# Flamingo block on one core: the opening reordered, the mask as a selection matrix, the hi and lo split of Wq by column blocks, K spread by SBUF-to-SBUF loads, the value projection in two halves

## The chip, the cores and the metric

One core of one Trainium2 chip. A core has TensorE (matmuls, here PE, with the loading of its stationary operand as PEld), VectorE (DVE), ScalarE (ACT), GpSimd (POOL) and SyncE (SP), each with its own queue of instructions, and 16 engines that move data (DMA). SyncE and ScalarE issue all transfers here. The metric is the device time of one execution in microseconds, lower is better. Before the change it is 689.58 us, the median of three runs (688.52 to 692.12).

## The reference

The block adds a gated cross attention and then a gated feed-forward part to `x`, which is 2 batches of 2048 rows of 512. The context is 77 rows of 384 for each batch, with a mask over these 77 rows.

```
q = (layernorm(x) @ Wq)   k = (context @ Wk)   v = (context @ Wv)    # 16 heads of 32
scores = einsum('bhid,bhjd->bhij', q, k) * scale
scores = where(context_mask, scores, -finfo.max);  attn = softmax(scores)
x = x + tanh(g_xattn[0]) * (einsum('bhij,bhjd->bhid', attn, v) @ Wo)
xq = fake_quant(layernorm(x));  gate = xq @ quant(w_gate).T;  up = xq @ quant(w_up).T
h = fake_quant(silu(gate) * up)
x = x + tanh(g_ffn[0]) * (h @ quant(w_down).T)
```

## The kernel before

The kernel has three blocks, one after the other: attention (to about 413 us), gate and up projection (to about 599 us), and down projection. The change lies in the opening of the first.

Attention works on 32 tiles of 128 rows. A matmul with full precision is made of three: each operand is split into a rounded part and the rest (`_hi`, `_lo`), and `three` multiplies hi by hi, hi by lo and lo by hi. For each tile of x, VectorE makes the statistics (`stats_both`), GpSimd the factors (`deviation`), ScalarE the normalised row (`normalise`), TensorE its transposes (`x_transpose`), and ScalarE and VectorE take these apart into hi and lo (`x_part`). `queries(m, t, part)` works on two tiles together, and for one column block of Wq at a time: tile number 0 does blocks 0 and 1, number 1 blocks 2 and 3. `q_part` splits what comes out.

Each engine's work is an order written out by hand: an opening, and then `tile_slots`, which runs `slot` once for each tile. In slot n TensorE does the scores of tile n, the transposes of the probabilities of tile n-1 and its outputs, queries for tile n+2, transposes of x for tile n+4, and the projection of tile n-2. Engines wait for one another by semaphores only.

The opening prepares keys and values. `c_sb` is the context, `cT` its transposes (L869), `cK` a version for the keys in which every masked row is replaced by the first row that is kept (L648 to L674; then a masked row's score is no larger than the maximum, and its value is made zero by `keepT`). The keys are 12 matmuls into `p_k` (L876). K stands in the scores as a block matrix, `k_hi` and `k_lo`, zero except for each head's own 32 rows; GpSimd fills both with zeros (L379, L380), ScalarE writes eight blocks of `k_hi` (L475) and VectorE eight of `k_lo` (L692). The values (L886) are scaled by the gate and by `keepT` into `v_sb` (L704), and SyncE spreads them by twelve loads from SBUF to SBUF into `vblk` (L323), which GpSimd has filled with zeros (L381).

`v_sb` lies in the buffer `pT`, into which ScalarE copies the transposed probabilities. So ScalarE waits for all twelve loads in slot 1, ahead of those copies:

```
if isinstance(n, int) and n == 1:
    act.wait_ge(l_v, 16 * SLOT0[KB])
```

The order of TensorE in the opening is: transposes of the context, 24 matmuls that keep it busy (`keep_warm`), keys, transposes of tiles 0 and 1, both halves of the values, queries for tiles 0 and 1, transposes of tiles 2 and 3, slots. SyncE issues, in this order, the context, x tiles 0 and 1, Wk, Wq, x tiles 2 and 3, Wv, x tiles 4 to 7, the first rows of w_gate (`rows(0)`), then after its waits the twelve loads into `vblk`, `rows(1)`, Wo and x tiles 8 to 11. ScalarE issues the mask and the four gates, each spread over 128 partitions, ahead of its first work.

## Time and profile before

| | |
|---|---|
| median of three runs | 689.58 us (688.52 to 692.12) |
| span of the profiled execution | 689.8 us; nothing is listed around it, so this is taken as its own time |
| mean granted TensorE clock | 0.983 of full speed |
| busy share of the span | PE 94%, PEld 72%, DVE 74%, ACT 52%, POOL 24% |
| DMA, mean over the span | 77 GB/s |

The profile is of one execution. Its page gives the busy time of each engine, a timeline in 40 slices, the DMA queues, the chain of work that ended last, and the costliest groups of instructions. An engine's busy share is a mean over stages with different limits; a matmul's busy time overlaps that of the next. Times in the rows are microseconds from the start of the span.

### The profile page before, as it was taken

Reading aid. Unit: us, or ns where it says so; the run is one execution under the profiler, and the core shown is the slowest. Engines: PE = TensorE matmul, PEld = TensorE weight load, DVE = VectorE, ACT = ScalarE, POOL = GpSimd, SP = SyncE. Lnnn points to the kernel's source line nnn. Section 1 sums busy time; section 2 is a strip of 40 time slices with the busy share of each in tenths; the row PEclk is TensorE's granted clock in tenths of the full one; section 3 lists DMA queues with packets and bytes.
Section 4 is the critical chain, followed back from the end, with each engine's and each line's share of the span. In section 5 each row is a group of like instructions: output and inputs, shape, how many; then the busy total and the mean of one; then the engine's idle time right before and its main releaser. Section 6 shows DMA issues by size and latency. Waiting matters only on the chain. (4 is left out here: it accounts for less than half of the span.)

```text
span 689.8 us, 13450 instructions
## 1 busy us (share of the span) xinstructions
PE 649.7 (94%) x4207; PEld 493.7 (72%) x4233; DVE 509.4 (74%) x943; ACT 357.2 (52%) x561; POOL 166.9 (24%) x376
## 2 busy tenths in 40 slices
PE   6789999999999999999999992999999999898997
PEld 6588999999999999999999981444444444343443
DVE  4687878787878878777767652799778878846664
ACT  1555555555555655454543433578666664345553
POOL 5122223222222322211101110111111110026775
PEclk9999999999999999999999997799999999998999
DMA  7258000001010100000000004041244000089723
GB/s 233 75 169 321 32 17 27 21 15 30 15 30 15 30 15 31 2 1 1 1 1 1 1 1 167 1 168 58 111 169 167 0 0 1 21 304 322 284 106 122
DMA packets 22488, 53.29 MB, mean 77 GB/s; under 512 B 4884, under 2 KB 5038, under 8 KB 22446
## 3 DMA queue, kind: packets, MB, share of 16 engines
q1 hardware_dynamic: 16654, 35.96, 14.5%
q10 hardware_dynamic: 5792, 16.80, 6.9%
q8 instruction: 23, 0.38, 0.2%
q14 instruction: 19, 0.16, 0.1%
HBM read 32.50 MB, written 19.92 MB: 76 GB/s over the span
## 5 line engine op out<-in xcount | busy, mean ns | idle before, releaser
L523 DVE TENSOR_REDUCE sb_smax<-ps_s 128x8 f32<-128x616 f32 x64 | 51.1, 798 | 64.6 <-PE ps_s L760 64.4
L1150 PE MATMUL ps_g<-sb_xqT,sb_wgu 128*128 128x512 bf16 x338 | 90.0, 385 | 1.2 <-DVE sb_xqT L1122 0.5
L1150 PE MATMUL ps_u<-sb_xqT,sb_wgu 128*128 128x512 bf16 x349 | 90.8, 382 | 0.2
L1039 ACT ACTIVATE sb_silu<-ps_g,sb_sgu 128x512 f32<-128x512 f32 x88 | 60.5, 687 | 57.1 <-PE ps_g L1150 48.4
L1313 PE MATMUL ps_z<-sb_wdT,sb_hq 128*128 128x512 bf16 x344 | 78.8, 389 | 4.8 <-ACT sb_hq L1246 4.4
L422 ACT COPY sb_pT<-ps_p 128x512 f32<-128x512 f32 (+1 forms) x96 | 46.4, 521 | 70.1 <-PE ps_p L771 70.1
L1111 DVE SCALAR_TENSOR_TENSOR sb_h<-ps_u,sb_sgu,sb_silu 128x512 f32<-128x512 f32 (+1 forms) x88 | 66.0, 750 | 20.8 <-PE ps_u L1150 20.0
L721 PE MATMUL ps_q<-sb_xT_hi,sb_wq_hi 128*128 128x256 f32 x256 | 77.5, 303 | 2.0 <-DVE sb_q_lo L514 1.5
L782 PE MATMUL ps_o<-sb_vblk,sb_pT 128*128 (+4 forms) x640 | 79.0, 270 | 0.1
L782 PEld LDWEIGHTS ps_o<-sb_vblk,sb_pT 128*128 128x128 f32 (+1 forms) x640 | 76.8, 191 | 0.6 <-ACT sb_pT L422 0.3
L723 PE MATMUL ps_q<-sb_xT_hi,sb_wq_lo 128*128 128x256 f32 x256 | 72.4, 283 | 0.0
L722 PE MATMUL ps_q<-sb_xT_lo,sb_wq_hi 128*128 128x256 f32 x256 | 72.3, 282 | 0.0
L1313 PEld LDWEIGHTS ps_z<-sb_wdT,sb_hq 128*128 128x128 bf16 x352 | 35.0, 100 | 48.6 <-ACT sb_hq L1246 5.4
L1115 DVE TENSOR_REDUCE sb_hmax<-sb_h 128x1 f32<-128x512 f32 (+1 forms) x88 | 60.4, 686 | 7.6
L1150 PEld LDWEIGHTS ps_u<-sb_xqT,sb_wgu 128*128 128x128 bf16 x352 | 34.7, 99 | 42.5 <-issue 1.7
L1246 ACT CAST sb_hq<-sb_h 128x1408 bf16<-128x1408 int8 x32 | 43.6, 1365 | 40.9 <-DVE sb_h L1266 40.9
L410 ACT CAST sb_oT_hi<-ps_x 128x512 fp32r<-128x512 f32 x31 | 18.2, 588 | 88.6 <-PE ps_x L805 88.6
L1231 POOL TENSOR_TENSOR sb_wgu<-sb_wgu,sb_x 128x512 f32<-128x512 f32 x31 | 51.3, 1661 | 34.3 <-DVE sb_wgu L1272 17.6
L1150 PEld LDWEIGHTS ps_g<-sb_xqT,sb_wgu 128*128 128x128 bf16 x352 | 33.1, 99 | 34.7 <-issue 1.8
L529 DVE TENSOR_TENSOR sb_prob<-ps_s,sb_smax 128x616 f32<-128x616 f32 x64 | 51.1, 798 | 3.0
L721 PE MATMUL ps_y<-sb_wo_hi,sb_oT_hi 128*128 128x512 f32 x124 | 51.3, 414 | 0.9 <-DVE sb_wo_lo L605 0.9
L721 PEld LDWEIGHTS ps_q<-sb_xT_hi,sb_wq_hi 128*128 128x128 f32 x256 | 48.8, 191 | 2.8 <-issue 1.9
(154 smaller groups left out, 1373.8 us busy)
## 6 DMA issues: line engine op xcount, KB each, us to landing
h_spill<-sb_h SPq DMA_DIRECT2D x4, 2816.0 KB, 8.4
sb_h<-h_spill ACTq DMA_DIRECT2D x16, 704.0 KB, 6.0
out_dram<-sb_wgu SPq DMA_DIRECT2D x32, 256.0 KB, 2.0
sb_x<-in_x_dram ACTq DMA_DIRECT2D x1, 4096.0 KB, 15.6
sb_w_in<-in_L_ffn_w_gate_dram SPq DMA_DIRECT2D x11, 256.0 KB, 2.8
sb_w_in<-in_L_ffn_w_up_dram SPq DMA_DIRECT2D x11, 256.0 KB, 2.6
sb_h<-in_L_ffn_w_down_dram SPq DMA_DIRECT2D x4, 704.0 KB, 6.3
sb_x<-in_x_dram SPq DMA_DIRECT2D x2, 1024.0 KB, 11.8
```

Of the source, the lines that this page charges most:

```text
L523: dve.tensor_reduce(smax[:, half, :].rearrange("p (g h) -> p g h", g=2), half_scores(), X, ALU.max).then_inc(v_max, 1)
L529: dve.tensor_tensor(prob[t % 2][:, half, :].rearrange("p (g h m) -> p g h m", g=2, h=HG), half_scores(), smax[:, half, :].rearrange("p (g ...
L721: pe.matmul(o, hi, rhi, start=first, stop=False)
L722: pe.matmul(o, hi, rlo, start=False, stop=False)
L723: return pe.matmul(o, lo, rhi, start=False, stop=last)
L782: last = pe.matmul(p_o[:, first:end + 1, :].rearrange("p h d -> p (h d)"), pT[rows, half * KB + j, :], vblk[rows, span(b), half, SLOT0[j]: ...
L1039: act.activation(silu[(j * KI + i) % 2][:, :, :].rearrange("p t n -> p (t n)"), p_g[(j * KI + i) % 2][:, :], ACT.Silu, scale=sgu[:, i:i + ...
L1111: dve.scalar_tensor_tensor(steps_h, p_u[(j * KI + i) % 2][:, :, :], sgu[:, KI + i:KI + i + 1], silu[(j * KI + i) % 2][:, :, :], ALU.mult, ...
L1115: dve.tensor_reduce(hmax[:, span(u)], steps_h, mybir.AxisListType.XY, ALU.max, apply_absolute_value=True).then_inc(v_hmax, 1)
L1150: last = pe.matmul(banks[(j * KI + i) % 2][:, :], wgu[:, what, k, i * P:(i + 1) * P], xqT[j][:, k, :], start=(k == 0), stop=(k == KD - 1))
L1231: pool.tensor_tensor(yd[k], yd[k], x1[:, span((v + RT) % NT), :].rearrange("p a d -> p (a d)"), ALU.add).then_inc(g_out, 1)
L1313: last = pe.matmul(p_z[k % 4][:, :], hq[k % 4][:, i, :], wdT[:, i, :], start=(i == 0), stop=(i == KI - 1))
```

## The change

x tiles 0 and 1 are loaded ahead of the context. The mask comes in as one row, is spread over the partitions by a matmul with a row of ones (`p_m`), and transposed by two matmuls (`p_mT`); from both VectorE builds a 77 by 77 selection matrix for each batch (`pickw`), and TensorE multiplies the context by it to get `cK`. The four gates come in as one row as well and are spread by a matmul. ScalarE copies `cT`. GpSimd makes the ramps, and it fills `k_lo` and `vblk` with zeros only after the factors of tiles 0 and 1. Wq is split in four column blocks. The K halves are written whole into `kc_hi` and `kc_lo`, by one instruction each, and eight loads from SBUF to SBUF put them into `k_hi` and `k_lo`. The transposes of tile 1 stand between the halves of the keys. The values' first half stands between the queries of tile 0 and of tile 1, behind the transposes of tile 2; the second half behind the transposes of tile 3, at the end of the opening. The statistics of tile 3 move ahead on VectorE.

```diff
...
+kc_hi, kc_lo = [spare[:, (5 + 4 * i) * B * M:(9 + 4 * i) * B * M].bitcast(F32R)
+                .rearrange("p (b g m) -> p b g m", b=B, g=KD) for i in range(2)]
...
+p_ck = p_p[0][:, :, :].rearrange("p k n -> p (k n)")[:, 0:KC * B * M]\
+    .rearrange("p (k b m) -> p k b m", k=KC, b=B)
+p_m = p_ob[:, 0:B * M].rearrange("p (b m) -> p b m", b=B)
+p_mT = p_ob[0:M, 2 * P:2 * P + B]
+p_gate = p_ob[:, 3 * P:3 * P + 4]
...
+    sp.dma_start(x1[:, 0:2, :], x_v[:, 0:2, :]).then_inc(l_x[0], 16)
...
-    sp.dma_start(x1[:, 0:2, :], x_v[:, 0:2, :]).then_inc(l_x[0], 16)
...
+    sp.wait_ge(g_zero, 8)
+    for kc, k_blk, done in ((kc_hi, k_hi, a_khi), (kc_lo, k_lo, v_klo)):
+        sp.wait_ge(done, 1)
+        for j in range(HG):
+            rows_j = slice(HD * j, HD * j + HD)
+            sp.dma_start(k_blk[rows_j, :, :, M * j:M * j + M].bitcast(F32).rearrange("p b g m -> p (b g) m"),
+                         kc[rows_j, :, :, :].bitcast(F32).rearrange("p b g m -> p (b g) m")).then_inc(l_k, 16)
...
-    sp.wait_ge(g_zero, 9)
...
-    pool.iota(ramp_i[:, :, :], [[0, B], [-1, M]], M, 0).then_inc(g_zero, 1)
+    pool.memset(ones_row, 1.0).then_inc(g_ramp, 1)
+    pool.memset(eps[:, :], EPS).then_inc(g_zero, 1)
+    pool.iota(ramp_i[:, :, :], [[0, B], [-1, M]], M, 0).then_inc(g_ramp, 1)
+    pool.iota(rampT_i, [[0, 1]], M, -1).then_inc(g_ramp, 1)
...
-    pool.memset(eps[:, :], EPS).then_inc(g_zero, 1)
...
+    pool.wait_ge(g_ramp, 3)
+    pool.tensor_copy(ramp[:, :, :], ramp_i[:, :, :]).then_inc(g_ramp, 1)
+    pool.tensor_copy(rampT, rampT_i).then_inc(g_ramp, 1)
...
+    pool.wait_ge(g_zero, 6)
+    for n in range(2):
+        deviation(n, n)
...
-    pool.wait_ge(g_zero, 9)
-    for n in range(5):
+    for n in range(2, 5):
...
-            act.wait_ge(v_wq, 1)
+            act.wait_ge(v_wq, KD)
...
-    act.dma_start(mask_u[:, :, :], mask.rearrange("(a b) m -> a b m", a=1)
-                  .broadcast_to([P, B, M])).then_inc(l_mask, 16)
-    for b in range(B):
-        act.dma_start(maskT_u[:, b:b + 1], mask[b:b + 1, :].rearrange("b m -> m b"))\
-           .then_inc(l_maskT, 16)
+    act.dma_start(mask_u, mask.rearrange("(a b) m -> a (b m)", a=1)).then_inc(l_mask, 16)
...
-        act.dma_start(gates[:, i:i + 1], bcast(a)).then_inc(l_small, 16)
+        act.dma_start(gate_row[:, i:i + 1], a.rearrange("(a n) -> a n", a=1)).then_inc(l_small, 16)
+    act.wait_ge(g_zero, 2)
+    act.activation(sg_e[:, 0:1], eps[:, :], ACT.Exp).then_inc(a_dummy, 1)
+    act.wait_ge(t_c, 1)
+    act.copy(cT, p_c).then_inc(a_c, 1)
...
+    x_part(1, 1)
...
-    act.copy(wq_hi[:, :, :], wq_raw).then_inc(a_wq, 1)
-    x_part(1, 1)
-    act.wait_ge(l_small, 64)
-    act.activation(tg[:, :], gates[:, 0:2], ACT.Tanh).then_inc(a_tg, 1)
-    act.activation(sg_e[:, :], gates[:, 2:4], ACT.Exp, scale=-1.0).then_inc(a_tg, 1)
+    for g in range(KD):
+        cols = slice(g * P, (g + 1) * P)
+        act.copy(wq_hi[:, :, cols], wq_raw[:, :, cols]).then_inc(a_wq, 1)
...
-    act.wait_ge(g_zero, 7)
-    for j in range(HG):
-        for i in range(2):
-            act.copy(k_hi[HD * j:HD * j + HD, :, 2 * i:2 * i + 2, M * j:M * j + M],
-                     p_k[HD * j:HD * j + HD, i, :, 0:B * M]
-                     .rearrange("p g (b m) -> p b g m", b=B)).then_inc(a_khi, 1)
+    act.copy(kc_hi.rearrange("p b (i g) m -> p i g b m", i=2),
+             p_k[:, :, :, 0:B * M].rearrange("p i g (b m) -> p i g b m", b=B)).then_inc(a_khi, 1)
+    act.wait_ge(t_gate, 1)
+    act.wait_ge(a_dummy, 1)
+    act.activation(tg[:, :], p_gate[:, 0:2], ACT.Tanh).then_inc(a_tg, 1)
+    act.activation(sg_e[:, :], p_gate[:, 2:4], ACT.Exp, scale=-1.0).then_inc(a_tg, 1)
...
-    q_part(1, 1)
...
+    q_part(1, 1)
...
-    dve.wait_ge(t_c, 1)
-    dve.tensor_copy(cT, p_c).then_inc(v_c, 1)
...
-    dve.wait_ge(g_zero, 2)
-    dve.tensor_copy(keep[:, :, :], mask_u[:, :, :]).then_inc(v_mask, 1)
-    dve.tensor_copy(ramp[:, :, :], ramp_i[:, :, :]).then_inc(v_mask, 1)
-    self_done(2)
-    dve.tensor_tensor(ramp[:, :, :], ramp[:, :, :], keep[:, :, :], ALU.mult).then_inc(v_mask, 1)
-    dve.tensor_scalar(drop[:, :, :], keep[:, :, :], -1.0, 1.0, ALU.mult, ALU.add).then_inc(v_mask, 1)
-    self_done(3)
-    dve.tensor_reduce(rank[:, :], ramp[:, :, :], X, ALU.max).then_inc(v_mask, 1)
-    dve.wait_ge(v_c, 1)
-    dve.tensor_tensor(cK, cT, by_chunk(keep), ALU.mult).then_inc(v_mask, 1)
-    self_done(5)
-    dve.tensor_tensor(first[:, :, :], ramp[:, :, :], rank[:, :].unsqueeze(2).broadcast_to([P, B, M]),
-                      ALU.is_equal).then_inc(v_mask, 1)
-    dve.tensor_scalar(none[:, :], rank[:, :], 0.0, None, ALU.is_equal).then_inc(v_mask, 1)
-    self_done(7)
-    dve.tensor_tensor(first[:, :, :], first[:, :, :], keep[:, :, :], ALU.mult).then_inc(v_mask, 1)
-    self_done(9)
-    dve.tensor_tensor(pick, cT, by_chunk(first), ALU.mult).then_inc(v_mask, 1)
-    self_done(10)
-    dve.tensor_reduce(c_0[:, :, :], pick, X, ALU.add).then_inc(v_mask, 1)
-    self_done(11)
-    dve.tensor_tensor(pick, c_0[:, :, :].unsqueeze(3).broadcast_to([P, KC, B, M]), by_chunk(drop),
-                      ALU.mult).then_inc(v_mask, 1)
-    self_done(12)
-    dve.tensor_tensor(cK, cK, pick, ALU.add).then_inc(v_ck, 1)
+    dve.tensor_copy(mask_row, mask_u).then_inc(v_row, 1)
+    dve.wait_ge(g_ramp, 5)
+    dve.wait_ge(t_m, 1)
+    dve.tensor_tensor(rampk[:, :, :], p_m, ramp[:, :, :], ALU.mult).then_inc(v_mask, 1)
+    dve.tensor_copy(kept[:, :], p_mT).then_inc(v_mask, 1)
+    dve.tensor_scalar(drop[:, :, :], p_m, -1.0, 1.0, ALU.mult, ALU.add).then_inc(v_mask, 1)
+    dve.wait_ge(v_mask, 1)
+    dve.tensor_reduce(rank[:, :], rampk[:, :, :], X, ALU.max).then_inc(v_mask, 1)
...
-    dve.wait_ge(l_maskT, 16 * B)
-    dve.tensor_copy(keepT[:, :], maskT_u[:, :]).then_inc(v_mask, 1)
-    self_done(13)
-    dve.tensor_tensor(keepT[:, :], keepT[:, :], none[0:M, :], ALU.add).then_inc(v_mask, 1)
+    dve.wait_ge(v_mask, 4)
+    dve.tensor_scalar(rankT[:, :], kept[:, :], rampT[0:M, :], None, ALU.mult).then_inc(v_mask, 1)
+    dve.tensor_scalar(none[:, :], rank[:, :], 0.0, None, ALU.is_equal).then_inc(v_mask, 1)
+    for b in range(B):
+        dve.tensor_scalar(pickw[0:M, b, :], identf[0:M, 0:M], kept[:, b:b + 1], None, ALU.mult)\
+           .then_inc(v_mask, 1)
+    dve.wait_ge(v_mask, 6)
+    dve.tensor_tensor(firstT[:, :], rankT[:, :], rank[0:M, :], ALU.is_equal).then_inc(v_mask, 1)
+    dve.tensor_tensor(keepT[:, :], kept[:, :], none[0:M, :], ALU.add).then_inc(v_mask, 1)
+    dve.wait_ge(v_mask, 9)
+    dve.tensor_tensor(firstT[:, :], firstT[:, :], kept[:, :], ALU.mult).then_inc(v_mask, 1)
+    dve.wait_ge(v_mask, 11)
+    for b in range(B):
+        dve.scalar_tensor_tensor(pickw[0:M, b, :], drop[0:M, b, :], firstT[:, b:b + 1],
+                                 pickw[0:M, b, :], ALU.mult, ALU.add).then_inc(v_pick, 1)
+    dve.wait_ge(t_ck, 1)
+    dve.tensor_copy(cK, p_ck).then_inc(v_ck, 1)
...
-    dve.wait_ge(a_wq, 1)
-    dve.tensor_tensor(wq_lo[:, :, :], wq_raw, wq_hi[:, :, :].bitcast(F32),
-                      ALU.subtract).then_inc(v_wq, 1)
...
-    dve.wait_ge(g_zero, 8)
-    for j in range(HG):
-        for i in range(2):
-            rows, cols = slice(HD * j, HD * j + HD), slice(M * j, M * j + M)
-            dve.wait_ge(a_khi, 2 * j + i + 1)
-            dve.tensor_tensor(k_lo[rows, :, 2 * i:2 * i + 2, cols],
-                              p_k[rows, i, :, 0:B * M].rearrange("p g (b m) -> p b g m", b=B),
-                              k_hi[rows, :, 2 * i:2 * i + 2, cols].bitcast(F32),
-                              ALU.subtract).then_inc(v_klo, 1)
+    for g in range(KD):
+        cols = slice(g * P, (g + 1) * P)
+        dve.wait_ge(a_wq, g + 1)
+        dve.tensor_tensor(wq_lo[:, :, cols], wq_raw[:, :, cols], wq_hi[:, :, cols].bitcast(F32),
+                          ALU.subtract).then_inc(v_wq, 1)
+    dve.wait_ge(a_khi, 1)
+    dve.tensor_tensor(kc_lo.rearrange("p b (i g) m -> p i g b m", i=2),
+                      p_k[:, :, :, 0:B * M].rearrange("p i g (b m) -> p i g b m", b=B),
+                      kc_hi.bitcast(F32).rearrange("p b (i g) m -> p i g b m", i=2),
+                      ALU.subtract).then_inc(v_klo, 1)
...
-    dve.wait_ge(a_tg, 2)
-    self_done(14)
-    for b in range(B):
+    stats_both(3)
+    x_part(2, 2)
+    def values(b):
...
-    dve.wait_ge(v_v, 2 * B)
-    dve.memset(p_p[1][:, 0, :], 0.0).then_inc(v_zero, 1)
-    stats_both(3)
+    dve.wait_ge(a_tg, 2)
+    values(0)
...
-    x_part(2, 2)
...
+    values(1)
+    dve.wait_ge(v_v, 2 * B)
+    dve.memset(p_p[1][:, 0, :], 0.0).then_inc(v_zero, 1)
...
-    pe.wait_ge(g_id, 1)
-    pe.wait_ge(l_ctx, 16)
-    for k in range(KC):
-        for b in range(B):
-            last = pe.transpose(p_c[:, k, b, :], c_sb[:, b, k * P:(k + 1) * P], identf[0:M, 0:M])
-    last.then_inc(t_c, 1)
-    keep_warm(24)
-    pe.wait_ge(v_ck, 1)
-    pe.wait_ge(l_wk, 16)
-    for g in range(KD):
+    def keys_part(g):
...
-    x_transpose(0)
-    x_transpose(1)
-    pe.wait_ge(l_wv, 16)
-    for b in range(B):
+    def values_part(b):
...
-    pe.wait_ge(v_wq, 1)
-    for m in range(2):
-        queries(m, m, 0)
-        queries(m, m, 1)
+    pe.wait_ge(g_id, 1)
+    keep_warm(4)
+    pe.wait_ge(g_ramp, 1)
+    pe.wait_ge(v_row, 1)
+    pe.matmul(p_m.rearrange("p b m -> p (b m)"), ones_row, mask_row, start=True, stop=True)
+    for b in range(B):
+        last = pe.matmul(p_mT[:, b:b + 1], mask_row[:, b * M:(b + 1) * M], ones_row[:, 0:1],
+                         start=True, stop=True)
+    last.then_inc(t_m, 1)
+    keep_warm(6)
+    pe.wait_ge(l_ctx, 16)
+    for k in range(KC):
+        for b in range(B):
+            last = pe.transpose(p_c[:, k, b, :], c_sb[:, b, k * P:(k + 1) * P], identf[0:M, 0:M])
+    last.then_inc(t_c, 1)
+    pe.wait_ge(l_small, 64)
+    pe.wait_ge(v_mask, 3)
+    pe.matmul(p_gate, ones_row, gate_row, start=True, stop=True).then_inc(t_gate, 1)
+    keep_warm(4)
+    x_transpose(0)
+    pe.wait_ge(v_pick, B)
+    for k in range(KC):
+        for b in range(B):
+            last = pe.matmul(p_ck[:, k, b, :], c_sb[:, b, k * P:(k + 1) * P], pickw[0:M, b, :],
+                             start=True, stop=True)
+    last.then_inc(t_ck, 1)
+    pe.wait_ge(v_ck, 1)
+    pe.wait_ge(l_wk, 16)
+    keys_part(0)
+    keys_part(1)
+    x_transpose(1)
+    keys_part(2)
+    keys_part(3)
+    for part in range(2):
+        pe.wait_ge(v_wq, part + 1)
+        queries(0, 0, part)
...
+    pe.wait_ge(a_c, 1)
+    pe.wait_ge(l_wv, 16)
+    values_part(0)
+    for part in range(2):
+        pe.wait_ge(v_wq, part + 3)
+        queries(1, 1, part)
...
-    pe.wait_ge(v_klo, 2 * HG)
+    values_part(1)
+    pe.wait_ge(l_k, 16 * 2 * HG)
...
```

The bodies of `keys_part`, `values_part` and `values` are the loops that stood in place before. Semaphore names, the other buffers' places in `spare` and the removed helpers `self_done`, `by_chunk` and `bcast` are left out of the diff.

## Rows read from the trace of the kernel before

**Rows 1.** The page's part 1: busy us (share of the span) xinstructions.

```profile
PE 649.7 (94%) x4207; PEld 493.7 (72%) x4233; DVE 509.4 (74%) x943; ACT 357.2 (52%) x561; POOL 166.9 (24%) x376
```

**Rows 2.** Windows: stretch, its length, busy us (x) of each engine, PEclk, DMA share, GB/s.

```profile
40.00:60.00 20.00, 18.58 (x156) 17.78 (x154) 16.63 (x35) 12.17 (x21) 4.46 (x16) 1.00 0.77 262
...
80.00:100.00 20.00, 20.00 (x154) 19.05 (x154) 17.04 (x38) 11.20 (x20) 5.56 (x19) 1.00 0.10 27
```

**Rows 3.** Timeline, PE: start, us, line, op, out<-in, shape, count, idle before.

```profile
6.13 1.00 PE L869 MATMUL ps_y<-sb_identf,sb_prob 77*128 77x77 f32 x6 [6.13 <-DMA sb_prob<-in_ctx_dram]
...
14.46 3.31 PE L876 MATMUL ps_s<-sb_prob,sb_x 128*128 128x154 f32 x24
...
20.17 5.31 PE L886 MATMUL ps_p<-sb_x,sb_prob 128*77 128x512 f32 x12
...
29.84 0.36 PE L721 MATMUL ps_q<-sb_xT_hi,sb_wq_hi 128*128 128x256 f32 x1 [1.49 <-DVE sb_q_lo L514]
...
32.79 0.60 PE L729 MATMUL ps_x<-sb_identf,sb_xn 128*128 128x128 f32 x4
...
35.42 0.38 PE L758 MATMUL ps_s<-sb_k_hi,sb_q_hi 128*128 128x308 f32 x1
...
45.60 1.22 PE L782 MATMUL ps_o<-sb_vblk,sb_pT 128*128 128x66 f32 x10
...
623.21 3.17 PE L1313 MATMUL ps_z<-sb_wdT,sb_hq 128*128 128x512 bf16 x7 [3.60 <-ACT sb_hq L1246]
```

**Rows 4.** Timeline of ACT, 19 to 45 us.

```profile
19.45 1.89 ACT L466 CAST sb_wq_hi<-sb_x 128x2048 fp32r<-128x2048 f32 x1
...
30.01 0.82 ACT L392 ACTIVATE sb_xn<-sb_x,sb_nb,sb_rs 128x512 f32<-128x512 f32 x1 [1.04 <-POOL sb_nb L344]
...
44.06 1.06 ACT L422 COPY sb_pT<-ps_p 128x512 f32<-128x512 f32 x2
```

**Rows 5.** Timeline of DVE, 7 to 31 us.

```profile
7.17 0.64 DVE L645 COPY sb_prob<-ps_y 128x462 f32<-128x462 f32 x1 [5.37 <-PE ps_y L869]
...
12.57 0.69 DVE L491 BATCH_NORM_STATS2 sb_bn<-sb_x 128x6 f32<-128x512 f32 x1
...
21.37 2.29 DVE L684 TENSOR_TENSOR sb_wq_lo<-sb_x,sb_wq_hi 128x2048 fp32r<-128x2048 f32 x1 [1.81 <-ACT sb_wq_hi L466]
...
24.18 3.54 DVE L692 TENSOR_TENSOR sb_k_lo<-ps_s,sb_k_hi 32x308 fp32r<-32x308 f32 x8
...
28.48 0.18 DVE L494 BATCH_NORM_AGGREGATE sb_mv<-sb_bn 128x2 f32<-128x6 f32 x1
...
30.40 0.80 DVE L704 TENSOR_SCALAR sb_pT<-ps_p,sb_tg,sb_wgu 77x512 f32<-77x512 f32 x1
```

**Rows 6.** Timeline of SyncE's queue: DMA issues of Wq and into vblk.

```profile
2.18 1.87 SPq L311 DMA_DIRECT2D sb_x<-in_L_xattn_Wq_dram  x1
...
31.32 10.38 SPq L323 DMA_DIRECT2D sb_vblk<-sb_pT  x12
```

**Rows 7.** The page's part 6, DMA issues: xcount, KB each, median us to landing.

```profile
out_dram<-sb_wgu SPq DMA_DIRECT2D x32, 256.0 KB, 2.0
```

**Rows 8.** Timeline of POOL, 1.8 to 6.1 us.

```profile
1.81 2.15 POOL L379 MEMSET sb_k_hi<- 128x2464 f32 x1
...
3.89 2.15 POOL L380 MEMSET sb_k_lo<- 128x2464 f32 x1
```

**Rows 9.** DMA view of 0 to 60 us: KB each, median us from issue to landing.

```profile
sb_x<-in_L_xattn_Wq_dram SPq DMA_DIRECT2D x1, 1024.0 KB, 13.7
...
sb_gates<-in_L_ffn_clip_down_dram ACTq DMA_DIRECT2D x1, 0.5 KB, 8.7
```

**Rows 10.** Windows of 1 us in the opening, and one of the last block.

```profile
9.00:10.00 1.00, 1.00 (x7) 1.00 (x6) 0.97 (x5) 0.00 (x0) 0.00 (x0) 1.00 1.05 395
...
12.00:13.00 1.00, 1.00 (x11) 1.00 (x10) 0.99 (x2) 0.00 (x0) 0.00 (x0) 1.00 0.57 150
...
625.00:630.00 5.00, 5.00 (x15) 1.83 (x14) 2.06 (x3) 1.69 (x3) 2.60 (x2) 0.58 0.96 356
```

33 lines of the change are left out of this document (17 added, 16 removed).

## The prediction

> **What bounds the kernel now.** I read the page's part 1 first: TensorE is busy for 94% of the span [rows 1], so what moves the end is time in which TensorE has nothing to do. The chain of waits on the page reaches back only into the last tenth of the span, so it says nothing of the opening. The windows show where TensorE is not full: in 80 to 100 us it is busy 20.00 of 20 us, in 40 to 60 us 18.58 [rows 2]. From about 46 us on, the slots follow one another on TensorE; the change ends before that. So the whole question is at what time TensorE reaches a fixed piece of work early in the steady part, and that piece must lie behind every wait that the opening can still cause.
>
> The timelines of the single engines give that piece. Slot 0 begins on TensorE with the scores at 35.42. But two slots' work later there is one more wait on the opening: in slot 1 ScalarE waits for `l_v` (the twelve loads that spread the values into `vblk`) before it copies the first transposed probabilities, at 44.06, because those copies overwrite `v_sb`. The first outputs on TensorE stand at 45.60 and wait for those copies [rows 3, 4]. The change does not touch this wait. I therefore compute two times: when TensorE enters slot 0, and when `vblk` is filled.
>
> The twelve loads are issued by SyncE from 31.32 for 10.38 us, so to 41.70, at 0.87 us each, right behind the last of the values on VectorE (30.40 + 0.80, then a copy of 0.17 us that overlaps it in part) [rows 5, 6]. The last of them landed after 41.70 and before 44.06. A transfer of 256 KB takes 2.0 us from issue to landing at the median [rows 7]; with the last issue beginning near 40.9 and a little more for its small pieces I take 43.1. So ScalarE had 44.06 - 43.1 = 0.96 us to spare. The two copies end at 45.12 and TensorE uses them at 45.60: another 0.48. The filling of `vblk` can come 1.44 us later at no cost; each us beyond costs a us.
>
> A rule of the Trainium skill bears on this slack. "DMA: Bandwidth & Descriptors", section "Anatomy of one DMA", gives each transfer a fixed cost of about 2.0 us beside its bytes. Counted from the end of the last issue that puts the landing at 43.7, the slack at 0.84 and the result 0.6 us later than below. The row of 2.0 us from issue to landing for 256 KB speaks for less than that.
>
> **The change, step by step, in times of the new opening.**
>
> *First loads.* The transfer that is issued first was there at 6.13 [rows 3]. The issue of Wq at 2.18 took 1.87 us and ended with GpSimd's first large memset (1.81 to 3.96); a second ran to 6.04 [rows 6, 8]. The change puts `k_lo` and `vblk` behind the second deviation, so only one such memset, some 2.7 to 4.9, lies on the first issues. x is now first and larger (512 KB for 231 KB): I take 6.0 for x and 6.8 for the context. From both sides: not before 4, and x was there by 12.57, when the statistics began without an idle wait [rows 5]. Wq took 13.7 us from its issue, so it landed at 15.9 [rows 9]; I take it as no later.
>
> *Mask and gates.* The mask's twelve VectorE instructions on the K path (7.17 to 12.57, before the statistics) become four short ones before the statistics, which the wait for x hides, and nine small ones after it, which I estimate at 0.2 us each with their waits, 1.8 together, and which TensorE's `keep_warm` covers; at a third of the 0.64 us of a 462-wide one [rows 5] they would hardly differ. The gate transfers took up to 8.7 us to land, the last one until about 15.3 [rows 9]; each was spread over 128 partitions. Now each is one element. TensorE waits for all four before its first transposes of x. I take them as landed by 8 and the wait at nothing; from the other side, if they land as late as before, this is a rival below.
>
> *TensorE to the keys.* Context transposes 6.9 to 8.0; four `keep_warm` matmuls are eight instructions. In 9 to 10 us 7 instructions show, in 12 to 13 us 11 [rows 10]: the first is the 1.2 GHz level, the second 2.4, although the row's granted clock says 1.00 in both. At the lower level they take 1.7 us, to 9.9. Beside them x: statistics 0.87, then from the end of the aggregate (28.66) to the normalising (30.01) 1.35, and 0.82 for it [rows 4, 5], so 9.1. Transposes of tile 0 to 10.8. The product with the selection matrix, twelve instructions of 77 columns, is not in the trace; between 12 x 0.06 and 12 x 0.25 I take 1.5, to 12.3. Then the copy of `cK`, 0.64 as the like-sized copy: 13.0. Before, the keys began at 14.46, held by the 24 `keep_warm` [rows 3]: 1.5 us gained.
>
> *Keys and queries of tile 0.* The keys take 3.31, the transposes of tile 1 0.60, between them 0.3 of hand-over: to 17.2. ScalarE's cast of Wq was 1.89 [rows 4]; a quarter is about 0.5, beginning at 16.2 behind tile 1's cast; the first quarter's low part (2.29 / 4 = 0.6 [rows 5]) is there at 17.6. Then queries(0) run 17.6 to 20.5: 24 instructions from 29.84 to 32.8 before [rows 3], the second quarter ready ahead of need. The values no longer stand in front of them; before, they took 5.31 there [rows 3]. This is a gain of nearly 8 us at this point.
>
> *The hole.* It is not kept. The next thing on TensorE is the transposes of tile 2, and they need its statistics, which VectorE does after `kc_lo` (one instruction of 0.80, as the values' of like length, for eight of 3.54 us in all; ScalarE's eight become one too [rows 5]). Wq's last low part ends 19.4, `kc_lo` 20.2, statistics 21.05, then 1.35: normalised 22.4 to 23.2. TensorE stands from 20.5 to 23.3, 2.8 us, with both halves of the values behind the transposes in its queue.
>
> *The rest of the opening.* Transposes 0.6 (23.9); values, first half, 2.65; queries(1) 3.0; transposes of tile 3 0.6; values, second half, 2.65 (5.31 / 2); less 0.9 for the overlap of neighbours: 32.5. Slot 0 begins at 32.5 instead of 35.42, 2.9 us earlier. The eight loads that spread K are issued from 19.0 and 20.2, at 0.87 each like the twelve, to 26 and landed by 28.5; TensorE asks at 32.5, so they cost nothing. Without that cover each us counts. They also stand before the `vblk` loads on SyncE, and are through long before those can start.
>
> *The values' way out.* The second half now ends where slot 0 begins, and VectorE's two instructions for it follow: 33.45 instead of 31.32. The twelve loads end their issue at 43.8, land at 45.2; `rows(1)` behind them goes out 2.1 later too, at 43.9, and is wanted by VectorE at about 47, where it may hold it 0.9 us at a place where TensorE has 1.4 to spare. ScalarE reaches its wait near 41 and stands there; TensorE reaches the outputs near 42.6 and stands too.
>
> **The sum.** The filling is 33.45 - 31.32 = 2.13 later, less the slack of 1.44: +0.7 us. The 2.9 us won at slot 0 end in this stall. Added to the profiled execution's span, 689.8, it is 690.5; that span is 0.2 above the median 689.58, so I forecast **690.3 us**, no change (within 0.5%, 3.4 us, about the least a measurement of this kernel can tell).
> Bounds: the landing at either of its ends makes it -0.7 or +1.7. TensorE's arrival at the second half of the values moves it one for one: x and context as early as 4 us give -1.5, the product at 3 us +1.5. Forecast's own range 688.3 to 692.3.
>
> **Rivals.**
> 1. *The values are done sooner than I count.* The sum falls one for one with their second half: if that ends at 28.9 instead of 32.5, the result is 690.3 - 3.6 = **686.7**. It would take a normalising of tile 2 at 18.8, before the queries, so a VectorE that reaches these statistics ahead of Wq's low parts. For it: the start of the loads is held back by memsets in the present trace, and everything on x is early. Against: in VectorE's new order the statistics stand behind `kc_lo`, which hangs on all of Wq, landed at 15.9.
> 2. *TensorE stays at 1.2 GHz* (the slower side). The place is keys, selection and transposes from 10 to 17 us; at 12 us the present kernel has run TensorE without a break since 6.13, the new one has gaps around every mask, gate and copy wait. The keys' 24 instructions would take 3.3 us more and the small ones 0.8: everything after, `vblk` too, is later by that: 4.1 + 0.7, less what the stand before the queries hides (0.4), on 689.6: **694.0**. It decides from some 3 us of such time on. The same happens if the 2.8 us hole lowers it: in the last block a stretch shows 0.58 (mostly 1.2 GHz) behind a stand of 3.6 us [rows 3, 10]; the hole is shorter, so I hold it unlikely, and values at half speed would give the same 2 to 4 us. "TensorE: Matmul & The Clock Gate" of the Trainium skill says too that the low clock is the default that activity releases, and that idle gaps bring it back; this trace agrees in the instruction counts.
> 3. *The gates land late.* At 15.3 as before, TensorE's first transposes begin 5.7 us later and everything behind them 5.5; with the forecast's 0.7 that is 6.2 on 689.6, **696**. Against: one element instead of 128.
> 4. *The change has no effect on the end* because other work takes up the difference both ways: the forecast's number within 0.5.
>
> **Chances.** Forecast 0.46, rival 1 0.22 (not quite half of it beyond -3.4), rival 2 0.17 (most beyond +3.4), rival 3 0.05, rival 4 0.10. Faster by over 0.5%: 0.10, slower 0.19, same 0.71. The range that leaves two in ten out: 686.6 to 694.0.
>
> **What would show it.** In the new trace: keys begin near 13 us; queries(0) end near 20.5 and TensorE then stands until 23.3 for the normalising; slot 0's scores start near 32.5; the `vblk` loads start near 33.4; the copies of slot 1 start only near 45, and TensorE's wait for them before the first outputs is 3 to 4 us long. It is wrong if `vblk` loads start before 31.3, if no such wait shows, or if instruction counts per us stay at 7 after 13 us.

## The result and the profile after

The changed kernel takes 697.35 us, the median of seven runs (693.30 to 698.61); the kernel before 689.58 (688.13 to 692.12, seven runs). The ratio, taken over the runs and not from the two medians (these alone give 1.0113), is 1.0096, 95% interval 1.0068 to 1.0125: slower by 1%, outside the predicted 686.6 to 694.0. In a later, larger comparison the same kernel has a median of 694.55 (689.53 to 701.53, twelve runs) against 689.62, ratio 1.0068 (1.0038 to 1.0097). The slowest of these twelve, 701.53, counts as a slow run and is left out of the ratio; the median of the other eleven is 693.38. The first seven runs fall into two groups, 693.3 to 693.6 and 697.4 to 698.6, and the difference between them is part of the answer.

The profiled execution of the changed kernel took 698.37 us and has a span of 696.6, 1.8 less; the other runs show the same 1.8 between time and span. So the profiled execution of before, with its span of 689.8, took some 691.6, 2.0 above its median, and not 689.8 as I had taken it. The forecast loses nothing by that, since its +0.7 was in the end set against the median; where the 2.0 lie is shown at the end of this section. The page of after, part 1 (columns as before): TensorE has 8.7 us more of busy time with the same number of instructions.

```profile
PE 658.4 (95%) x4207; PEld 502.3 (72%) x4233; DVE 504.6 (72%) x938; ACT 356.3 (51%) x559; POOL 165.7 (24%) x380
```

TensorE's timeline, changed kernel: the product with the selection matrix (L912), keys (L877), queries (L731), transposes of tile 2 (L739), both halves of the values (L885), scores of slot 0 (L768) and the first two outputs (L792).

```profile
11.60 2.68 PE L912 MATMUL ps_p<-sb_wgu,sb_prob 77*128 77x77 f32 x12
...
15.01 3.45 PE L877 MATMUL ps_s<-sb_prob,sb_x 128*128 128x154 f32 x12 [0.73 <-DVE sb_prob L691]
...
19.10 2.28 PE L877 MATMUL ps_s<-sb_prob,sb_x 128*128 128x154 f32 x12
21.31 0.39 PE L731 MATMUL ps_q<-sb_xT_hi,sb_wq_hi 128*128 128x256 f32 x1
...
26.80 0.96 PE L739 MATMUL ps_x<-sb_identf,sb_xn 128*128 128x128 f32 x4 [2.35 <-ACT sb_xn L418]
27.55 4.18 PE L885 MATMUL ps_p<-sb_x,sb_prob 128*77 128x512 f32 x6
...
34.87 2.74 PE L885 MATMUL ps_p<-sb_x,sb_prob 128*77 128x512 f32 x6
37.04 0.71 PE L768 MATMUL ps_s<-sb_k_hi,sb_q_hi 128*128 128x308 f32 x1
...
51.43 2.40 PE L792 MATMUL ps_o<-sb_vblk,sb_pT 128*128 128x66 f32 x10 [3.95 <-ACT sb_pT L448]
...
58.33 1.23 PE L792 MATMUL ps_o<-sb_vblk,sb_pT 128*128 128x66 f32 x10
```

The same work took 3.31 for all keys, 5.31 for all values and 1.22 for an output [rows 3]. Here the keys take 5.73, the first half of the values 4.18 while the second takes 2.74, the first output 2.40 and the next 1.23: these are the two levels of TensorE's clock, 1.2 and 2.4 GHz, and stretches in which it changed from one to the other. SyncE's queue and ScalarE's wait, in two fences, show the way out of the values.

```profile
2.18 0.49 SPq L323 DMA_DIRECT2D sb_x<-in_L_xattn_Wq_dram  x1
...
22.67 2.74 SPq L334 DMA_DIRECT2D sb_k_hi<-sb_wgu  x4
25.46 2.59 SPq L334 DMA_DIRECT2D sb_k_lo<-sb_wgu  x4
...
38.57 10.28 SPq L342 DMA_DIRECT2D sb_vblk<-sb_pT  x12
```

```profile
50.30 1.07 ACT L448 COPY sb_pT<-ps_p 128x512 f32<-128x512 f32 x2 [4.41 <-DMA sb_vblk<-sb_pT]
```

The loads into `vblk` start 7.25 us later than the 31.32 of [rows 6]. The first output stands 5.83 later than the 45.60 of [rows 3]: 7.25 less 1.42. So the wait in slot 1 sets TensorE's time, and the slack was as predicted (1.44). In windows of the changed kernel (columns as in [rows 2]), the granted clock falls to 0.50, the 1.2 GHz level, behind each of the two gaps:

```profile
12.00:13.00 1.00, 1.00 (x6) 1.00 (x6) 0.00 (x0) 1.00 (x2) 0.97 (x1) 1.00 1.05 403
...
19.00:20.00 1.00, 1.00 (x6) 1.00 (x5) 0.03 (x1) 0.65 (x2) 0.00 (x0) 1.00 0.00 0
...
28.00:29.00 1.00, 1.00 (x2) 0.25 (x1) 0.59 (x1) 1.00 (x2) 0.00 (x0) 0.50 0.59 122
...
52.00:57.00 5.00, 5.00 (x25) 4.91 (x25) 2.71 (x7) 1.01 (x3) 0.16 (x2) 0.50 1.00 375
```

The first two rows are the opening, with 6 matmuls in the microsecond at 12 and at 19 us, where the kernel before already had 11 at 12 us [rows 10]. The clock column says 1.00 in both. The counts are a hint only, since they are of matmuls of different widths (77, 154 and 128 columns). What tells the level is the time of the same work in two executions: the product takes 2.68 us here and 1.46 in experiment 1, the first half of the keys 3.45 and 1.84.

One more account begins at the second output of the kernel before:

```profile
49.49 1.22 PE L782 MATMUL ps_o<-sb_vblk,sb_pT 128*128 128x66 f32 x10
```

From the first to the second output the kernel before took 3.89 us (49.49 - 45.60), the changed one 6.90. That is another 3.01 at the low level, so at the second output it is 5.83 + 3.01 = 8.84 late. The spans differ by 6.8, and the traces show where the other 2.0 us are. Up to the end of attention nothing changes (its last transposes stand 8.9 later, at 415.8 for 406.9). At the change of blocks the kernel before spends 0.6 us more up to the first transposes of the gate and up projection (437.9 for 429.7) and 1.4 more in the low level behind them. This is likely the scatter of single executions and not an effect of the change, though no second profile of the kernel before shows it: from the second output to the end the twelve profiles of this document take 637.7 to 640.3 us, the kernel before 640.3, a variant of it (experiment 3) 639.7 and one of the changed kernel (experiment 5) 639.9. With 638.5, the median of the twelve, its execution would have taken 689.8, within 0.2 of its median.

### The profile page after: what moved, and what is told of

It is laid out like the page before. It is cut to its first block and busy times, and to the rows that moved or that the text cites. A ratio compares the mean times of both kernels' runs of the same rounds, so it can differ in the third digit from the quotient of the medians.

```text
span 696.6 us, 13454 instructions
## 1 busy us (share of the span) xinstructions
PE 658.4 (95%) x4207; PEld 502.3 (72%) x4233; DVE 504.6 (72%) x938; ACT 356.3 (51%) x559; POOL 165.7 (24%) x380
## 5 line engine op out<-in xcount | busy, mean ns | idle before, releaser
L792 PE MATMUL ps_o<-sb_vblk,sb_pT 128*128 (+4 forms) x640 | 80.2, 273 | 4.0 <-ACT sb_pT L448 3.9
L792 PEld LDWEIGHTS ps_o<-sb_vblk,sb_pT 128*128 128x128 f32 (+1 forms) x640 | 77.8, 193 | 4.8 <-ACT sb_pT L448 4.4
L731 PE MATMUL ps_q<-sb_xT_hi,sb_wq_hi 128*128 128x256 f32 x256 | 77.9, 304 | 0.0
L731 PE MATMUL ps_y<-sb_wo_hi,sb_oT_hi 128*128 128x512 f32 x124 | 51.3, 413 | 1.0 <-DVE sb_wo_lo L627 1.0
L731 PEld LDWEIGHTS ps_q<-sb_xT_hi,sb_wq_hi 128*128 128x128 f32 x256 | 49.2, 192 | 0.4 <-issue 0.3
```

The source lines that it names most:

```text
L731: pe.matmul(o, hi, rhi, start=first, stop=False)
L792: last = pe.matmul(p_o[:, first:end + 1, :].rearrange("p h d -> p (h d)"), pT[rows, half * KB + j, :], vblk[rows, span(b), half, SLOT0[j]: ...
```

## The experiments

**1. The changed kernel again**, for a second profile and more runs. The source is the same.

> The changed kernel again, for a second profile beside the others. Its seven times fell in two groups, 693.3 to 693.6 and 697.4 to 698.6. The profile at hand is of the slower group and shows the 1.2 GHz level three times in the first 60 us: in the opening until about 20 us (6 to 7 TensorE instructions in a us), from 27.0 to 30.4 us behind a stand of 2.35 us, and from 50.9 to 57.7 us behind a stand of 3.95 us. Theory CLOCK (the low level is what costs): where a run lands in the faster group, its profile shows one of the latter two shorter or missing. Theory LOADS (the eight loads that spread K, and what they delay, cost the time): both groups have the same clock up to 60 us and differ in a transfer.

Measured 694.55 (ratio and range above). This profile (691.4 us of span, 693.18 in time) is of the lower group. TensorE, SyncE and a window of it:

```profile
10.12 1.46 PE L912 MATMUL ps_p<-sb_wgu,sb_prob 77*128 77x77 f32 x12
12.31 1.84 PE L877 MATMUL ps_s<-sb_prob,sb_x 128*128 128x154 f32 x12 [0.73 <-DVE sb_prob L691]
...
22.07 1.11 PE L739 MATMUL ps_x<-sb_identf,sb_xn 128*128 128x128 f32 x4 [2.35 <-ACT sb_xn L418]
22.98 3.78 PE L885 MATMUL ps_p<-sb_x,sb_prob 128*77 128x512 f32 x6
...
46.50 2.40 PE L792 MATMUL ps_o<-sb_vblk,sb_pT 128*128 128x66 f32 x10 [3.98 <-ACT sb_pT L448]
...
53.20 1.22 PE L792 MATMUL ps_o<-sb_vblk,sb_pT 128*128 128x66 f32 x10
```

```profile
33.60 10.30 SPq L342 DMA_DIRECT2D sb_vblk<-sb_pT  x12
```

```profile
8.00:9.00 1.00, 1.00 (x10) 0.90 (x9) 0.81 (x6) 0.68 (x2) 0.78 (x4) 1.00 1.04 393
...
46.00:52.00 6.00, 5.50 (x26) 5.41 (x27) 2.78 (x7) 1.39 (x4) 0.10 (x1) 0.50 0.98 366
```

The same program reached the high level at about 8 us (10 matmuls in that microsecond) instead of about 20. Its keys start 2.7 us sooner, its `vblk` loads 4.97 sooner. Here the loads began at 33.60 (predicted 33.45) and the first output stood at 46.50 (45.60 + 0.7 = 46.3), though on the way there errors cancel, as told below. What is left is the low level behind the stand, 6.70 us to the second output for 3.89. Neither theory came out as I had written it: both low stretches are there in this execution too and nearly as long, and the loads of K are the same in both (2.74 and 2.59 us of the queue there, 2.73 and 2.59 here); the difference lies in the opening.

So the two groups of times fit these two openings. With one profile in each group this is fitted and not shown, and the openings are not all that scatters: the twelve later times run from 689.5 to 701.5, and some lie between the groups or outside them. Of the seven profiles with this opening (those of both comparisons and of experiments 2, 4, 5, 6 and 10) six have the slow form and one the fast, though in the times the lower group is about as large as the upper.

**2. The values early**: both halves directly behind the queries of tile 0, ahead of the transposes of tile 2; VectorE's part likewise. All else stays as changed.

```diff
...
         queries(0, 0, part)
+    values_part(0)
+    values_part(1)
     x_transpose(2)
...
-    values_part(0)
     for part in range(2):
         queries(1, 1, part)
     x_transpose(3)
-    values_part(1)
...
```

> Both halves of the values stand right behind the queries of tile 0, in the hole, and VectorE takes them out there. Theory LATE VALUES (the second half at the end of the opening holds the vblk loads and thereby slot 1): the loads into vblk start near 30.5 us instead of 38.6, ScalarE does not wait for them in slot 1, no hole behind the queries of tile 0, no low level from 27 to 30 us nor from 51 to 58, slot 0 starts near 35; the time falls by about 8 us, to 689 to 690. Theory LOADS: it falls by 2 at most, since the eight loads for K are as before. Theory OPENING CLOCK alone: the keys still run at the low level until 20 us, so this one does not get below 689.

Measured **685.21 us** (684.45 to 688.40, seven runs), ratio 0.9929 (0.9911 to 0.9948). This beats both kernels by more than I expected (689 to 690). Its profiled execution, 688.40, is the slowest of the seven and had the slow opening; it is 10.0 us shorter than the profiled one of the changed kernel, which had the slow opening too. TensorE and SyncE:

```profile
24.29 5.31 PE L885 MATMUL ps_p<-sb_x,sb_prob 128*77 128x512 f32 x12
...
44.22 1.22 PE L792 MATMUL ps_o<-sb_vblk,sb_pT 128*128 128x66 f32 x10
48.11 1.23 PE L792 MATMUL ps_o<-sb_vblk,sb_pT 128*128 128x66 f32 x10
```

```profile
30.56 10.30 SPq L342 DMA_DIRECT2D sb_vblk<-sb_pT  x12
```

There is no gap before the transposes of tile 2, since the values fill it; no wait before the first output; and no stretch at the low level after either. One reordering removes all three costs.

**3. The kernel before with only the second half of the values moved** behind the transposes of tile 3, on TensorE and on VectorE.

```diff
...
+    values_part(0)
     for m in range(2):
         queries(m, m, 0)
         queries(m, m, 1)
     x_transpose(2)
     x_transpose(3)
+    values_part(1)
...
```

> The kernel before, with one thing of the change: the second half of the values stands behind the transposes of tile 3 on TensorE, and VectorE takes it out at the end of its opening. Nothing else of the change is in it. Theory LATE VALUES: the loads into vblk start at about 37 to 38.5 us instead of 31.3, ScalarE waits for them in slot 1 for about 4 us, TensorE stands for as long, the 1.2 GHz level follows for one or two stretches, and the total is 7 to 9 us more than before, 696.5 to 698.5: as slow as the whole change. Rival OTHER PARTS (the mask as a matrix, the loads of K, the opening's clock make the loss): it is at most 3 us slower than before.

Measured **698.55 us** (697.53 to 700.90, six runs), ratio 1.0124 (1.0098 to 1.0151). This one move is as dear as the whole change. TensorE, SyncE and ScalarE:

```profile
29.72 0.36 PE L725 MATMUL ps_q<-sb_xT_hi,sb_wq_hi 128*128 128x256 f32 x1 [2.02 <-DVE sb_q_lo L514]
...
52.06 1.69 PE L786 MATMUL ps_o<-sb_vblk,sb_pT 128*128 128x66 f32 x10 [4.05 <-ACT sb_pT L422]
57.65 1.22 PE L786 MATMUL ps_o<-sb_vblk,sb_pT 128*128 128x66 f32 x10
```

```profile
39.08 10.38 SPq L323 DMA_DIRECT2D sb_vblk<-sb_pT  x12
```

```profile
50.93 1.07 ACT L422 COPY sb_pT<-ps_p 128x512 f32<-128x512 f32 x2 [4.52 <-DMA sb_vblk<-sb_pT]
```

The loads start 7.76 later, less 1.44 of slack gives 6.3; measured at the first output 6.46. Then 5.59 us to the second output instead of 3.89, 1.7 more at the low level. The gap of 2.02 us ahead of the second queries left the clock up: in 30 to 31 us the granted clock is 1.00, and each of these matmuls takes the 0.28 us that it takes elsewhere at the high level. Set beside experiment 2 this also prices the rest of the change: with the values early it gains 4.4 us (689.6 to 685.2); with the values late in both it gains 1.2 to 4.0 (698.55 to 697.35 or 694.55), which fits a wait that keeps most of it.

**4. The stand before the first output filled**: 18 matmuls of the identity, whose output nobody reads, ahead of the first output in slot 1.

```diff
...
+if isinstance(n, int) and n == 1:
+    for _ in range(18):
+        last = pe.matmul(p_y[:, 0:P], identf[:, :], identf[:, :], start=True, stop=True)
...
```

> 18 matmuls of 128 columns on the identity (36 instructions, 3.9 us) stand ahead of the first outputs in slot 1, where TensorE now stands 3.95 us for the loads into vblk. They write a PSUM bank that nothing uses then. Theory CLOCK: TensorE's first outputs start at the same 51.4 us, the low level from 50.9 to 57.7 us is gone, the work behind runs 3 us faster: total 3 us less in the runs that had the low level there (so 695 for the slower group, and little for the faster group). Rival STALL ONLY (only the stand itself costs): total the same within 0.5 us.

Measured 693.24 (688.87 to 697.45, twelve runs), ratio 1.0054 (1.0027 to 1.0080). Its profiled execution had the slow opening, as the one of the changed kernel, and the two can be set side by side:

```profile
47.34 4.18 PE L845 MATMUL ps_y<-sb_identf 128*128 128x128 f32 x36
51.46 1.33 PE L792 MATMUL ps_o<-sb_vblk,sb_pT 128*128 128x66 f32 x10
...
55.46 1.23 PE L792 MATMUL ps_o<-sb_vblk,sb_pT 128*128 128x66 f32 x10
```

The first output is where it was (51.43), the second 2.87 us sooner and the span 3.1 shorter (693.5). So the wait itself costs nothing beyond its length, but the clock lost in it costs 3 us more. The median moved by 1.3 only (0.1 against the eleven runs that count), and the intervals overlap: the 3 us are read from the two profiles and not from the times.

**5. The gap before the transposes of tile 2 filled** with 11 such matmuls.

```diff
...
+for _ in range(11):
+    last = pe.matmul(p_y[:, 0:P], identf[:, :], identf[:, :], start=True, stop=True)
...
 x_transpose(2)
...
```

The lines left out make these matmuls wait for ScalarE's copy of `cT`, as the values do, and signal their end.

> After the change, with 11 matmuls on the identity (22 instructions, 2.4 us at the high level) between the queries of tile 0 and the transposes of tile 2, where TensorE stands 2.35 us; they write a bank that is free. Theory CLOCK: the transposes of tile 2 start at the same time after the queries (2.3 to 2.5 us), there is no stretch at a granted 0.5 behind the hole, the first half of the values takes 2.7 us instead of 3.8 to 4.4, and the loads into vblk start 1.5 to 2.0 us sooner than without the matmuls: 36.7 us where the opening was slow, 31.8 where it was fast. The total falls by the same 1.5 to 2.0 us. Rival: the values are slow because ScalarE, VectorE and the K loads read the same memories then; then the first half still takes 3.8 us or more, and nothing is gained.

```profile
24.29 2.62 PE L927 MATMUL ps_y<-sb_identf 128*128 128x128 f32 x22
...
27.29 2.74 PE L885 MATMUL ps_p<-sb_x,sb_prob 128*77 128x512 f32 x6
...
49.73 1.55 PE L792 MATMUL ps_o<-sb_vblk,sb_pT 128*128 128x66 f32 x10 [3.95 <-ACT sb_pT L448]
...
55.30 1.22 PE L792 MATMUL ps_o<-sb_vblk,sb_pT 128*128 128x66 f32 x10
```

```profile
36.87 10.28 SPq L342 DMA_DIRECT2D sb_vblk<-sb_pT  x12
```

TensorE's rows: values 2.74 instead of 4.18. SyncE's: loads 1.70 sooner. ScalarE, VectorE and the loads of K run beside the values as before, so the rival, that these slow the values down, is out. The price behind the unfilled stand has changed too: 5.57 us to the second output, as in experiment 3 (5.59), where the three profiles with a low stretch behind the hole take 6.70 to 6.95. So the two stretches are not independent; what links them is not shown. The second output is 3.03 sooner in all. But the median is 694.69 (693.78 to 698.10, six runs), ratio 1.0071 (1.0043 to 1.0100): against the changed kernel no gain can be read, with six runs of a kernel whose openings scatter by 5 us.

**6. Both fillers**, as a test of the whole account.

> The changed kernel with both fillers: 11 identity matmuls in the gap before the transposes of tile 2 and 18 in the stand before the first outputs. Theory (the failed step is the clock in these two places; late vblk costs what was predicted): no low stretch from the hole on, first half of the values 2.7 us, outputs(0,1) about 4.9 us sooner than in the changed kernel's profile (1.7 from the hole, 3.1 from the stand), median 689.5 to 692, close to the predicted 690.3 and to the kernel before. Rival (the low clock is only a record, or the two medians of -1.3 and +0.1 add up as they stand): 693 to 694.5.

Measured **690.25 us** (688.91 to 695.62, twelve runs), ratio 1.0029 (1.0005 to 1.0052). TensorE, and a window:

```profile
27.29 2.74 PE L889 MATMUL ps_p<-sb_x,sb_prob 128*77 128x512 f32 x6
...
49.73 1.33 PE L792 MATMUL ps_o<-sb_vblk,sb_pT 128*128 128x66 f32 x10
...
53.72 1.22 PE L792 MATMUL ps_o<-sb_vblk,sb_pT 128*128 128x66 f32 x10
```

```profile
52.00:57.00 5.00, 4.41 (x38) 4.00 (x36) 4.36 (x10) 4.25 (x8) 0.74 (x2) 1.00 0.84 301
```

The granted clock is 1.00 where it was 0.50. The second output is 4.61 sooner than in the changed kernel (expected 4.9). The median is 690.25, beside a forecast of 690.3, but it lies at the upper edge of a lower group and is not the time of one kind of run. Its interval is clear of the one of the changed kernel's first comparison (1.0068 to 1.0125) and overlaps that of the second (1.0038 to 1.0097). The single runs say more: seven of twelve are at or below 690.3, against one of the changed kernel's nineteen. Seven runs are at 688.9 to 690.3, one at 692.3, four at 694.0 to 695.6: the opening still has its two forms. The profiled one, 694.37, had the slow one.

**7 to 10. Smaller questions.** Twelve `keep_warm` matmuls instead of four ahead of the transposes of tile 0, in three kernels, to have the high level in every opening; and the kernel of experiment 2 with K written into `k_hi` and `k_lo` directly, as before the change.

```diff
...
-    keep_warm(4)
+    keep_warm(12)
     x_transpose(0)
...
```

In the changed kernel:

> Twelve instead of four keep_warm matmuls ahead of the transposes of tile 0 (16 more instructions, 2 to 3.5 us of TensorE). Theory CLOCK: the count rises from 7 to 11 instructions in a us near 13.5 us instead of 20, the keys take 3.3 us in all instead of 5.7, and queries of tile 0 start 1 to 2 us sooner than 21.3 in spite of the 2 to 3 us put in. The vblk loads then start 1 to 2 us sooner and the total is 1 to 2 us less. Rival SMALL WORK (the opening is slow because its many small matmuls are bound by their issue, not by the clock): everything behind is 2 to 3 us later and the total 2 to 3 us more, counts stay at 6 to 7.

In experiment 2's:

> The kernel with early values (685.2 us), with twelve instead of four keep_warm matmuls ahead of the transposes of tile 0. With the late values this brought the 2.4 GHz level at about 11 us in place of 20 and queries of tile 0 about 1.5 us sooner than in a slow opening, but 3.6 us later than in an opening that was fast anyway. Theory CLOCK LOTTERY: the same here; against the slow openings of the early values 1 to 1.5 us less, against its fast ones more, so the spread of the runs gets narrower and the median moves by less than 1 us either way. Rival: the opening's clock decides all, and the median falls by 1.5 us or more.

With both fillers:

> The one before with 12 instead of 4 keep_warm matmuls ahead of the transposes of tile 0, so that the opening too should be at 2.4 GHz. Theory: spread of the runs smaller, the slow openings (up to 5 us later at vblk) gone, the median at most 1 us below the kernel with both fillers alone, since the 12 matmuls cost about 1 us of the opening themselves: 689 to 691.5. Rival (the opening's level does not reach the end): the same within 0.5.

The medians of the three are 696.16 (693.62 to 698.60, six runs; ratio 1.0079, 1.0052 to 1.0107), 685.62 (682.95 to 687.78, seven; 0.9938, 0.9912 to 0.9964) and 693.02 (689.58 to 694.69, twelve; 1.0046, 1.0028 to 1.0064). All three profiles show the keys at the high level, the first of them so:

```profile
15.98 1.84 PE L877 MATMUL ps_s<-sb_prob,sb_x 128*128 128x154 f32 x12 [0.73 <-DVE sb_prob L691]
```

Yet these begin 0.97 later than in the changed kernel's slow opening and 3.67 later than in its fast one. The eight additional matmuls are sixteen instructions; the queries of tile 0 begin 1.05 sooner than in the slow opening (20.26 for 21.31) and 3.67 later than in the fast one (16.59). That the keys take 1.84 here rules out the rival that small matmuls are slow by themselves. The gain of 1 to 2 us that I expected in the changed kernel does not show in its times, and in experiment 2's kernel the runs did not draw together (4.8 us from lowest to highest, for 4.0). My expectation for the third, at most 1 us below experiment 6, was wrong: it is 2.8 above it. Only two of its runs are below 690.3, where experiment 6 has seven, and none is above 694.7, where experiment 6 has two: it seems to trade the good openings for middling ones.

> The kernel with early values (685.2 us), with the K blocks written directly again: eight casts on ScalarE (2.9 us) and eight differences on VectorE (3.5 us), no loads from SBUF to SBUF for K. Theory COVERED: VectorE reaches the statistics of tile 2 about 2.7 us later, but the values (5.3 us on TensorE) cover it, so the transposes of tile 2 start at most 0.5 us later and the total is 0 to 1 us more. Theory LOADS (the eight loads cost time by themselves): it is 1 us or more faster. Rival K CHAIN: the 2.7 us show in full, 687.9.

The last of the four is experiment 10. Its diff takes the eight loads out and puts the eight copies and eight subtractions of 32 rows back. TensorE (selection product, first output) and VectorE:

```profile
12.85 2.68 PE L914 MATMUL ps_p<-sb_wgu,sb_prob 77*128 77x77 f32 x12
...
45.77 1.22 PE L794 MATMUL ps_o<-sb_vblk,sb_pT 128*128 128x66 f32 x10
```

```profile
2.40 2.27 DVE L658 CAST sb_wgu<-sb_wgu 1x154 f32<-1x154 uint8 x1 [0.32 <-DMA sb_wgu<-in_mask_BxS_bf_dram]
...
24.23 3.55 DVE L702 TENSOR_TENSOR sb_k_lo<-ps_s,sb_k_hi 32x308 fp32r<-32x308 f32 x8
```

Median 687.41 (682.80 to 690.33, twelve runs), ratio 0.9952 (0.9927 to 0.9976). VectorE spends 3.55 us on `k_lo` where one instruction takes 0.79 in the changed kernel. In its profile the first output stands at 45.77, 1.55 later than in experiment 2's, but 1.25 of that was there already at the selection product (12.85 for 11.60). It comes from VectorE's first row: the cast of the mask took 2.27 us, where it takes 0.23 to 0.30 in the other profiles of this opening, and TensorE's first matmul on the mask waited 1.22 us for it. The loads of K have no part in that. So the K loads are worth 0.3 us by the profiles and 2.2 by medians whose intervals overlap; I take it as a small gain whose size is open.

## Why the prediction was wrong

*What bounds the kernel.* Right. The filling of `vblk` decides, through ScalarE's wait; experiment 3 moves it with nothing else of the change and pays for it one to one at the first output (7.76 less 1.44 is 6.3, measured 6.46).

*First loads, mask and gates.* Right. VectorE began the statistics of x at 5.66 without an idle wait (I took x as there at 6.0), and the gates' matmul stood at 8.36:

```profile
5.66 0.68 DVE L513 BATCH_NORM_STATS2 sb_bn<-sb_x 128x6 f32<-128x512 f32 x1
```

```profile
8.36 0.59 PE L906 MATMUL ps_o<-sb_wgu 1*128 1x4 f32 x2
```

Rival 3 is out.

*TensorE to the keys.* The failed step in the runs of the upper group. I took the product as 1.5 us and the keys as 3.31, that is, at 2.4 GHz. So it was in the second profile (1.46, and 1.84 + 1.74). In the first, all of it ran at 1.2 GHz until 20 us: product 2.68, keys 3.45 + 2.28. The keys began at 15.0 instead of 13.0, and the `vblk` loads, which I put at 33.45, began 5.1 us late. The sign I had named for it, counts that stay at 7 a microsecond after 13 us, is there (6). I had this as rival 2, at 694.0, but as one or the other outcome for all runs, where the same program did both; and its 694.0 falls short of the upper group mainly because it too has no price behind the stand.

*The hole.* The second failed step. Its place and cause were right (2.35 us, predicted 2.8). "The hole is shorter, so I hold it unlikely" that it lowers the clock was wrong. It did in both profiles: 4.18 and 3.78 us for the first half of the values. Filling it returned 1.70 us. The nearest row that I used, a stand of 3.6 us, bounded the matter from one side only; the 1.49 us gap ahead of the queries [rows 3], behind which the clock stayed up, was the other side, and 2.35 lay between them. (Experiment 3 later showed a gap of 2.02 with the clock still up, so the row that I lacked was a close one.)

*The rest of the opening.* Here a slip in the sum was hidden by luck. The terms behind the hole (0.6, 2.65, 3.0, 0.6, 2.65, less 0.9, from 23.3) give 31.9 for slot 0 and not the 32.5 that I wrote. Three other errors stand beside it. I let the loads start 0.95 us behind slot 0, where all profiles of the changed kernel show 1.53 (32.07 to 33.60, 37.04 to 38.57). In the execution of experiment 1 the transposes of tile 2 began 1.2 us sooner than forecast (22.07 for 23.3). And the low level in the values, which I had not counted, took 1.5. That the loads began at 33.60 for my 33.45 is the outcome of these four, and no sign that each was right.

*The values' way out.* The step that failed in every run without a filler. The chain, the slack and the length of the stand (3.95, predicted 3 to 4) were right. The last load landed 1.45 to 1.47 us after the end of its issue where ScalarE waited for it (48.85 to 50.30, 43.90 to 45.37), for the 1.4 that I took. The 2.0 that I had set beside it from the Trainium skill, "DMA: Bandwidth & Descriptors", section "Anatomy of one DMA — SWDGE (gpsimd) path", is given there for transfers that GpSimd issues, and SyncE issues these; the measured slack of 1.42 us decides. What was missing is a term of the sum: I priced the stand by its length alone. The low level behind it costs another 2.8 to 3.0 us here (6.70 and 6.90 to the second output for 3.89) and 1.7 in experiment 3. I had read that same pattern in the last block (0.58 behind 3.60) and did not apply it to the stall that I had forecast myself.

*The K loads.* Right that they cost nothing at this place, and each issue took 0.68 us for the 0.87 that I took.

Put together: 690.3, plus 0.2 at the first output, plus 2.8 behind it, is 693.3, and the lower group is at 693.3 to 693.6. With the 4.97 of the slow opening it is 698.3, and the upper group is at 697.4 to 698.6. The 0.2 holds the hole's low stretch of 1.5, cancelled as told above, so a fit to a few tenths is partly luck. Experiment 6 took out the two low stretches behind the gaps, and its lower seven runs are at 688.9 to 690.3. What isn't settled is what decides between the two openings: both executions have the same instructions and TensorE shows busy from 1.5 us on in both, up to a gap of 0.73 ahead of the keys.

Three things stay loose. The ratios of the changed kernel in the two comparisons (1.0096 and 1.0068) may differ by how many slow openings each drew; no profile of those runs shows it. The single fillers move the median less than the profile. And the part behind the second output scatters by 2.6 us from profile to profile, partly in the low level at the change of blocks, which hides effects of 1 to 2 us in single executions.

## What to carry to other kernels

A stall on TensorE has two prices, its length and the low clock behind it, and where a gap lies between one that kept the clock and one that lost it, both outcomes belong in the range. Work that another engine waits for goes first, and work with slack fills the gap: the values in the gap gave 685.21 us where the values behind it gave 694.55 to 697.35. Before an opening is judged by one profile, look at the spread of the runs; two groups 5 us apart want a profile each. And a landing within 0.2 us of the forecast is checked term by term before it counts as understood: here four errors had cancelled.
